# Two fused transformer layers on eight cores: first attention in query tiles of 256 with exponentials over three PSUM banks

## The reference, cut to what matters

```
# layer 0: full attention, 16 heads of 64, over all 4096 tokens of the sequence
q = quat_norm(quat_linear(x, qW, qb)); k = quat_norm(quat_linear(x, kW, kb)); v = quat_linear(x, vW, vb)
scores = einsum('bthd,bshd->bhts', q, k) * Dh ** -0.5 + mean(sin(J)) * 0.1
x = layernorm(x + quat_linear(softmax(scores) @ v, oW, ob))
# FFN: x and weight are quantized per block of 32 to fp6 (e2m3) with a block scale
x = layernorm(x + quantized(x) @ quantized(weight).T + bias)
# layer 1: windowed attention (256 keys), 16 heads on 2 key/value heads, then RWKV channel mixing
x = layernorm(x + local_attention(x) @ Wo + bo)
x = layernorm(x + sigmoid(xr @ Wr.T) * (square(relu(xk @ Wk.T)) @ Wv.T))
```

## Time and profile before

| | |
|---|---|
| median of 3 runs | 2056.3 us (2054.02 to 2269.13) |
| profiled execution | 2055.19 us; span of its slowest core 2053.7 us (cores 2044.7 to 2053.7) |
| TensorE busy | 1815.6 us, 88% of the span |
| ScalarE busy | 1616.9 us, 79% |
| VectorE busy | 1067.1 us, 52% |
| GpSimd busy | 406.4 us, 20% |
| stage B, 1088 steps | 1154 us |
| bridge | 134 us |
| stage C | 454 us |

### The profile page before, as it was taken

The page is one execution under the profiler, slowest core; times in us unless marked ns, Lnnn a source line. Parts: engine busy times, 40 slices in busy tenths (PEclk is TensorE's granted clock), DMA queues, the critical chain, the costliest instruction groups (busy, mean ns, idle before and its releaser), DMA issues.

```text
span 2053.7 us, 43415 instructions; the slowest of 8 cores (2044.7 to 2053.7 us)
## 1 busy us (share of the span) xinstructions
PE 1815.6 (88%) x14874; PEld 809.2 (39%) x15022; DVE 1067.1 (52%) x1568; ACT 1616.9 (79%) x2212; POOL 406.4 (20%) x271
## 2 busy tenths in 40 slices
PE   4999998888888989989989989899888799999995
PEld 2444444333222323323223322233345465556553
DVE  5655652476232244622254423464384568888873
ACT  2344339999999999999999999999624677887872
POOL 3000000000001000110000100001010267766775
PEclk9999999999999999999999999999999699999998
DMA  7323211100411010020101112202633301111111
GB/s 103 83 41 73 41 31 56 40 27 6 131 42 60 6 44 22 19 78 4 47 4 37 41 38 42 53 17 61 157 60 75 73 23 43 43 51 45 43 43 42
DMA packets 59731, 100.01 MB, mean 49 GB/s; under 512 B 21489, under 2 KB 42097, under 8 KB 58114
## 3 DMA queue, kind: packets, MB, share of 16 engines
q1 hardware_dynamic: 37010, 66.72, 10.0%
q0 software_dynamic: 22512, 30.51, 8.7%
HBM read 88.86 MB, written 22.02 MB: 54 GB/s over the span
## 4 chain that ended last, share of the span: by engine, by line
ACT 43%; PE 31%; issue 16%; DVE 6%; POOL 1%; DMA 1%; ACTq 1%; DVEq 0%; POOLq 0%
ACT TE L756 40%; PE PALL L1155 13%; PE PALL L1295 7%; PE PALL L1262 2%; PE PALL L1332 2%; PE PALL L1342 1%; PE PALL L1211 1%; PE PALL L1313 1%; DMA TE<-XF 1%; DVE SMALL L1102 1%; DVE TY L1089 1%; ACTq L755 1%; POOL TY L679 1%; PE PALL L1377 1%; DVE TY L1035 1%
## 5 line engine op out<-in xcount | busy, mean ns | idle before, releaser
L756 ACT ACTIVATE TE<-PALL,BIASB 128x1024 bf16<-128x1024 f32 x1088 | 1131.9, 1112 | 22.1 <-PE PALL L1168 11.9
L1168 PE MATMUL PALL<-TE,TY 64*128 64x512 bf16 (+1 forms) x2560 | 425.6, 351 | 117.0 <-ACT TE L756 115.7
L1184 PE MATMUL PALL<-TE,TY 128*64 128x512 bf16 (+1 forms) x2560 | 339.1, 357 | 0.7 <-ACT TE L756 0.7
L1193 PE MATMUL PALL<-TE,TY 128*64 128x512 bf16 x2176 | 325.7, 379 | 0.0
L1168 PEld LDWEIGHTS PALL<-TE,TY 64*128 64x128 bf16 x2560 | 123.0, 93 | 513.0 <-issue 511.5
L1028 DVE COPY TY<-PALL 128x512 f32<-128x512 f32 (+1 forms) x40 | 24.5, 612 | 345.3 <-PE PALL L1193 345.3
L771 ACT ACTIVATE TY<-PALL,SMALL 128x384 bf16<-128x384 f32 x272 | 155.9, 584 | 48.1 <-DVE SMALL L1063 47.5
L703 ACT ACTIVATE TX<-PALL,BIASB 128x512 f32<-128x512 f32 (+1 forms) x104 | 66.2, 658 | 148.4 <-PE PALL L1155 147.0
L611 POOL TENSOR_TENSOR TX<-TX 128x1024 f32<-128x1024 f32 x17 | 40.0, 2356 | 657.1 <-DVE TY L954 657.1
L1155 PE MATMUL PALL<-TE 128*128 128x512 bf16 (+1 forms) x692 | 143.9, 368 | 21.5 <-DMA TE<-XF 20.8
L1193 PEld LDWEIGHTS PALL<-TE,TY 128*64 128x64 bf16 x2176 | 120.3, 110 | 107.4 <-issue 7.3
(11 more groups left out here) (136 smaller groups left out, 2277.3 us busy)
## 6 DMA issues: line engine op xcount, KB each, us to landing
TE<-WOD SPq DMA_DIRECT2D x5, 2048.0 KB, 8.1
TX<-XST SPq DMA_DIRECT2D x17, 512.0 KB, 3.4
TY<-Y2SP POOLq DMA_DIRECT2D x17, 512.0 KB, 3.5
YOUT<-TY SPq DMA_DIRECT2D x17, 512.0 KB, 2.6
TE<-FWD SPq DMA_DIRECT2D x4, 2048.0 KB, 9.7
Y2SP<-TY SPq DMA_DIRECT2D x17, 256.0 KB, 2.0
TE<-XF POOLq DMA_DIRECT2D x8, 512.0 KB, 10.2
TY<-XF POOLq DMA_DIRECT2D x8, 512.0 KB, 9.4
```

The costliest lines, as they stand in the source:

```text
L756: s.activation(EXPS(m), PB(2 * (m % 2), 0, 1024), AF.Exp, bias=BIASB[:, 63:64], scale=0.125).then_inc(*up("exp", m))
L1168: op = t.matmul(PB(2 * (m % 2) + hh, x * w, w), KB(c, (s * k + x) * 128, 128, 64 * hh, 64), QB(c, 0, w, 64 * hh, 64), start=True, stop=Tru ...
L1184: t.matmul(PB(6, 0, w)[64 * hh:64 * hh + 64, :], VB((s + d) * k + x, (2 * c + hh) * 64, 64), EXPS(m + d)[:, hh * 512 + x * w:hh * 512 + x ...
L1193: op = t.matmul(PB(7, 0, 512)[64 * hh:64 * hh + 64, :], ONEB, EXPS(m + d)[:, hh * 512:hh * 512 + 512], start=(first and d == 0), stop=(las ...
```

## The change

- Queries of layer 0's attention go in nine tiles: one of 128 and eight of 256. Stage A keeps the old tiles under the name `ATILES`.
- The work is cut into 2176 units of 512 score columns (with 256 queries: 128 keys, both heads). A step is three units, 1536 columns in three banks (0 to 2, and 3 to 5), and one exponential; there are 726 steps. `EXPS` is a ring of 4.
- `scores(m)` has six matmuls of 256 columns. Unit 2 of a step has both of its heads in one bank; its second head waits, on the counter `third`, until the first one's matmul is complete.
- Numerators and denominators share bank 6 (256 columns each); `pv` goes by units. When the last unit of a (tile, c) is through, the rest of that iteration's units is put off to the next iteration (`pv_plan`).
- The products have one bank, 7, in stage B. Both chunks' first halves are done, then both chunks' second halves; `z1` and `z2` are done by half. `quant` is done in two parts. WB is loaded in halves of 1 MB, each as soon as that half has been used for the last time. Q tiles are loaded two tiles ahead, into two sets of buffers.
- `att_out` copies both parts in one instruction of 512 columns.
- The last tile has two chunks, so the bridge has two, and the last 512 tokens' `pre` are done as blocks of 256, 128 and 128.

```diff
-TILES = [(2048, 128), (0, 512), (512, 512), (1024, 512), (1536, 512)]
-STEPS = [(T, c, s) for T, (a, w) in enumerate(TILES) for c in range(8) for s in range(32 * w // 512)]
-NST = len(STEPS)
-RING = 6
+TILES = [(2048, 128)] + [(256 * i, 256) for i in range(8)]
+BUNITS = [(T, c, k) for T, (a, w) in enumerate(TILES) for c in range(8) for k in range(32 * w // 256)]
+NB = len(BUNITS)
+NST = (NB + 2) // 3
+RING = 4
+def pv_plan():
+    out, at, cut = {}, 0, False
+    for n in range(NST + 8):
+        avail = min(3 * (n - 1), NB)
+        if n % 2:
+            end = avail
+        elif cut:
+            end = min(3 * (n - 2), NB)
+        else:
+            end = max([u + 1 for u in range(at, avail) if is_last(u)], default=at)
+        cut = False
+        while at < end and not cut:
+            out.setdefault(n, []).append(at)
+            cut = is_last(at)
+            at += 1
+    return out
...
+    def tile(T, s):
+        n = TILES[T][1] // 128
+        for j in range(n):
+            put("sp", max(s - 24, 0), "xld", T, j)
+            put("pool", s - 2, "xb", T, j)
+            for nh in (0, 1):
+                e = s + 8 * (n * nh + j)
+                for i in range(4):
+                    put("pe", e + 2 * i, "o", T, j, 4 * nh + i)
+                put("dve", e + 7, "z1", T, j, nh)
+            put("act", e + 11, "r1", T, j)
+            put("dve", e + 12, "n1", T, j)
+        f = s + 16 * n + (6 if n == 2 else 14)
+        quant(T, 0, f - 9.5, f - 6.5)
+        if n == 2:
+            quant(T, 1, f + 4, f + 9.5)
+        for j in range(n):
+            ffn(T, j, f + 18 * j)
+        for nh in (0, 1):
+            put("sp", s + 8 * n * (nh + 1) - 1, "wld", T, "f", nh)
+            put("sp", f + 18 * n - 9 + 8 * nh, "wld", T + 1, "o", nh)
...
+    for T in range(L):
+        s = max(free, BASE[T + 1] + 8)
+        s += s % 2
+        free = tile(T, s) + (12 if T == 0 else 4)
...
+        def cols_of(u, hh):
+            return ((0, 512), (256, 768), (1024, 1280))[u % 3][hh]
...
-                s.activation(EXPS(m), PB(2 * (m % 2), 0, 1024), AF.Exp, bias=BIASB[:, 63:64], scale=0.125
+                s.activation(EXPS(m), PB(3 * (m % 2), 0, 1536), AF.Exp, bias=BIASB[:, 63:64], scale=0.125
...
             def scores(m):
                 if m >= 2:
                     t.wait_ge(*at("exp", m - 2))
-                for x in range(k):
-                    for hh in (0, 1):
-                        op = t.matmul(PB(2 * (m % 2) + hh, x * w, w), KB(c, (s * k + x) * 128, 128, 64 * hh, 64),
-                                      QB(c, 0, w, 64 * hh, 64), start=True, stop=True, tile_position=(64 * hh, 0))
+                for r, hh in (((2, 0), (0, 1), (0, 0), (1, 1), (1, 0), (2, 1)) if n == 3 else ((0, 0), (0, 1))):
+                    u = 3 * m + r
+                    T, c, k = BUNITS[u]
+                    w = TILES[T][1]
...
+                    if (r, hh) == (2, 1):
+                        t.wait_ge(*at("third", m))
+                    for x in range(256 // w):
+                        op = t.matmul(PB(3 * (m % 2), cols_of(u, hh) + x * w, w),
+                                      KB(c, (k * 256 // w + x) * 128, 128, 64 * hh, 64), QB(T, c, 64 * hh, 64),
+                                      start=True, stop=True, tile_position=(64 * hh, 0))
+                    if (r, hh) == (2, 0):
+                        op.then_inc(*up("third", m))
                 op.then_inc(*up("sc", m))
+            def pv(u):
+                if u % 3 == 0:
+                    t.wait_ge(*at("exp", m))
+                if k == 0 and u:
+                    t.wait_ge(*at("pvn", *BUNITS[u - 1][:2]))
+                for a in (0, 256):
+                    for x in range(256 // w):
+                        for hh in (0, 1):
+                            e = cols_of(u, hh) + x * w
+                            op = t.matmul(PB(6, a, w)[64 * hh:64 * hh + 64, :],
+                                          ONEB if a else VB(k * 256 // w + x, (2 * c + hh) * 64, 64), EXPS(m)[:, e:e + w],
...
             def att_out(T, c):
-                v.tensor_copy(NM, PB(6, 0, w)).then_inc(*up("pvn", T, c))
-                    op = v.tensor_copy(DN, PB(7, 0, w))
+                v.tensor_copy(MQ[:, 0:2 * w].rearrange("p (x q) -> p x q", q=w),
+                              PB(6, 0, 512).rearrange("p (x q) -> p x q", q=256)[:, :, 0:w]).then_inc(*up("pvn", T, c))
...
             for n in range(NST + 8):
                 if n < NST:
                     scores(n)
-                if n % 2 and 3 <= n < NST + 2:
-                    pv(n - 3)
+                for u in PVP.get(n, ()):
+                    pv(u)
                 beside(n)
```

More of the change, by code:

```diff
@@ L86, in b_plan @@
-    for k in range(8):
[L87 to L109, removed]
+    def quant(T, j, b, b2):
+        put("dve", b, "quant", T, j, 0)
+        put("dve", b2, "quant", T, j, 1)
+    def ffn(T, j, f):
+        put("pe", f, "t", T, j)
+        put("dve", f + 1, "tev", T, j)
+        put("pool", f + 1, "xf", T, j)
+        for i in range(8):
+            put("pe", f + 2 + 2 * i, "f", T, j, i)
+        put("dve", f + 9, "z2", T, j, 0)
+        put("dve", f + 17, "z2", T, j, 1)
+        put("act", f + 21, "r2", T, j)
+        put("dve", f + 22, "n2", T, j)
+        put("sp", f + 22, "y2", T, j)
@@ L110, in b_plan @@
+    for k in range(8):
+        b = 4 + 10 * k
+        quant("w", k, b, b + 3)
+        put("pe", b + 8, "t", "w", k)
+        put("dve", b + 9, "tev", "w", k)
+        put("sp", max(b - 30, 0), "fw", k)
+    put("sp", 86, "fwst")
+    for nh in (0, 1):
+        put("sp", 88, "wld", 0, "o", nh)
+    free = 108
+    for T in range(L):
+        s = max(free, BASE[T + 1] + 8)
+        s += s % 2
+        free = tile(T, s) + (12 if T == 0 else 4)
     B = BASE[L]
-    put("pool", B + 100, "w1qkv")
@@ L112, in b_plan @@
-    put("sp", B + 220, "x2", 4)
-    for i in range(2):
-        put("sp", B + 230, "x2", i)
+    put("pool", B + 12, "w1qkv")
+    for i, at in ((4, 34), (0, 44), (1, 55), (2, 66)):
+        put("sp", B + at, "x2", i)
     E = NST + 8
-    put("sp", E, "wld", L, "f")
-    put("sp", E + 1, "x2", 2)
-    put("pool", E + 1, "wk")
[L119 to L125, removed]
@@ L127, in last, with prep @@
-    def last(j, o, z1, n1, q, z2, n2):
-        put("pool", NST - 8 + 2 * j, "xb", L, j)
+    for j in (0, 1):
+        put("sp", B + 20, "xld", L, j)
+        put("pool", NST - 8 + 2 * j, "xb", L, j)
+    put("sp", E, "wld", L, "f", 0)
+    put("sp", E + 1, "x2", 3)
+    put("pool", E + 1, "wk")
+    put("pool", E + 13, "w1o")
+    put("pool", E + 50, "wr")
+    def prep(i, e, d):
+        for n in range(10):
+            put("pe", e + d * n, "pre", *i, n)
+            put("dve" if n == 1 else "act", e + d * n + 0.5, "prev", *i, n)
@@ L129, in last @@
+    def last(j, o, z1, n1, q, f, z2, n2):
         for i in range(8):
             put("pe", o + 0.1 * i, "o", L, j, i)
-        put("dve", z1, "z1", L, j)
+            put("pe", f + 1.5 + 0.1 * i, "f", L, j, i)
+        for nh in (0, 1):
+            put("dve", z1 + 0.1 * nh, "z1", L, j, nh)
+            put("dve", z2 + 0.1 * nh, "z2", L, j, nh)
         put("act", z1 + 2.6, "r1", L, j)
         put("dve", n1, "n1", L, j)
-        put("dve", q, "quant", L, j)
+        quant(L, j, q, q + 0.1)
         put("pool", q + 8, "xf", L, j)
-        put("pe", q + 8.6, "t", L, j)
@@ L137, in last @@
[L137 to L140, removed]
+        put("pe", f, "t", L, j)
+        put("act", f + 1, "tev", L, j)
         put("act", z2 + 3, "r2", L, j)
@@ L143, in last, with back @@
         put("sp", n2, "y2", L, j)
[L145 to L154, removed]
+    def back(j, e):
         put("pe", e, "yt", L, j)
         put("act", e + 0.4, "yte", L, j)
-        prep((3, j), [e + 0.5 + 0.45 * n for n in range(10)])
+    prep((4, -1), E, 0.5)
+    last(0, E + 5, E + 8.6, E + 13.2, E + 17.2, E + 30, E + 36, E + 41)
+    last(1, E + 9, E + 12.2, E + 17.4, E + 26, E + 38, E + 44, E + 49)
+    prep((0, -1), E + 13, 1.7)
+    prep((1, -1), E + 34, 1.8)
+    back(0, E + 53)
+    prep((2, -1), E + 54, 1.7)
+    back(1, E + 71)
+    prep((3, 0), E + 72, 0.9)
+    prep((3, 2), E + 82, 0.5)
+    prep((3, 3), E + 88, 0.5)
     for e in plan:
-        plan[e] = {it: plan[e][it] for it in sorted(plan[e])}
+        steps = {}
+        for it in sorted(plan[e]):
+            steps.setdefault(int(it) if it < NST + 8 else it, []).extend(plan[e][it])
+        plan[e] = steps
     return plan
@@ L468, in _ @@
             y.dma_start(out=OBD, in_=OBROW[0:1, :]).then_inc(*up("obd", by=16))
[L469 to L470 removed]
+            for i in range(NA):
+                a, w = ATILES[q_tile(i)]
                 for h in range(2):
```

345 lines of the change are left out of this document (169 added, 176 removed).

## The result

The changed kernel takes 2140.2 us (median of 4 runs) where the kernel before took 2055.5: the ratio is 1.041, with a 95% interval of 1.039 to 1.043. It is slower by more than 2%, to which the forecast gave 0.35 (0.43 went to "within 2%"), and 5 us above the stated range. The profiled execution took 2137.45 us against 2055.19, 82 more. (In some runs the cores of one die are granted a lower clock and take some per cent longer; the ratios leave these runs out, and the text goes by ratios.)

A forecast was written before the change was run, and what follows sets the result against it. TensorE was taken as the bound beside a product part, a ring between TensorE and ScalarE elsewhere. 2055.2 + 26 (steps) + 24 (hand-offs) + 11 (late copies) + 1 (stage B's start) - 32 (bridge) = 2085 us; range 1985 to 2135.

The forecast's parts named there:

- the stated range: Whole kernel: 1985 to 2135 us, taking in rival 2's value and the nearly free wait on third at 0.10.
- the ring of exponential and scores: Stage B without a product part: exponential, answer, scores, V and ones, next exponential set the pace, 3.07 us a pair of steps.
- ScalarE's floor of 2.88: Stage B: exponentials at a pitch of 1.44 us, 2.88 a pair of steps, reached neither with nor without a product part.
- V and ones: TensorE's V and ones matmuls in stage B: 12 pairs and changes of tiling, 1.43 us in two steps.
- The bridge: The part with two chunks less and the last 512 tokens' blocks: from 134 to 102 us, -32 (bounds -24 and -38).
- Transfers: WB moved in halves, 17 times instead of 9, and q loads a tile ahead: cost nothing.
- The wait on `third`: Last score matmul of each step in stage B: stalls TensorE 0.25 us (bounds 0 and 0.30), scores hold it 0.68.
- 1180 + 24 in the forecast: Stage B: 1180 us for 363 pairs of steps against 1154 before, plus 24 for punctual hand-offs of bank 6.
- the hand-off of bank 6: Stage B, before a c's first V matmul: TensorE waits for the bank's copy, +24 us (bounds 0 and 40), late copies +11.
- late copies: Bank 6's copy behind quant on VectorE, about one place a tile, and a tight first tile: +11 us (bounds 0 and 50).
- Rival 2: Bank 6's copy queued behind quant on VectorE costs 50 to 60 us in place of 11: 2130 us; chance 0.20.
- Rival 3: Narrow matmuls cost a fixed 0.02 us a pair, 18 pairs in two steps: +131, 2215 us; chance 0.03.

The follow-up runs named there:

- e7: The changed kernel with each exponential over 1024 of the step's 1536 columns: 2125 us in the best run, ratio 1.038 (1.021 to 1.054) to the kernel before.
- e4: The changed kernel without quant's rounding to the fp6 grid, four of six VectorE instructions of each half left out: 2055 us, ratio 1.000 to the kernel before.
- e2: The changed kernel with the copy out of bank 6 done by ScalarE instead of VectorE: about 2089 us, ratio 1.017 to the kernel before.
- e5: The changed kernel with VectorE's copy out of bank 6 in its own buffer, put between single instructions of quant: 2082 us, ratio 1.013 to the kernel before.
- e1: The changed kernel with units cut by head, one head to a bank, and no wait on third: 2091 us, ratio 1.018 to the kernel before.
- e3: The changed kernel with one head to a bank and the bank 6 copy done by ScalarE: 2040 us, ratio 0.993 to the kernel before.
- e6: The changed kernel with one head to a bank, VectorE's copy between single instructions, weight chunks every 12 steps instead of 10: 2027 us, ratio 0.987 to the kernel before.

## Why the prediction was wrong

**Steps that held.** With a product part beside the attention TensorE is the bound (e7 shortens the exponentials, and these pairs stay at 3.22 us). Without one the ring of exponential and scores is, as forecast: 3.07 forecast, 3.11 measured. The prediction also said that ScalarE's floor of 2.88 is reached in neither kind of stretch; about a third of the pairs without a product did reach it (2.86). V and ones take 1.43 a pair of steps. The bridge went from 134 to 100, forecast 102. Transfers: no wait of TensorE for a half of WB is in the list, though the bytes that SP's queue moved rose from 67 to 84 MB. The halves of WB cost nothing.

**The wait on `third`**: mechanism right, size a little over. It holds a score group to 0.63 us, not 0.68: the stall is 0.20, not 0.25, and a pair with a product takes 3.22, not 3.33. The steps with the punctual hand-offs, 1180 + 24 in the forecast, came to 1174. This error of 30 us was in the kernel's favour, and it hides a part of the next one.

**The step that failed is "the hand-off of bank 6"**, in its second term: late copies, put at 11 us with bounds 0 and 50. It measured 102, the excess of the 46 pairs of steps above. It was mis-sized in two ways.
1. The late copies. I had seen that `att_out` could stand behind the second half of `quant`, in one place a tile, and called the first tile crowded. 20 copies were late: 8 up to 463 us, for 28 us of standing, and 12 in the tiles after, for 37. The normalization (line 1083) stands in that queue too, and no term had it; its 0.81 us were 2.8 in the five places of stage B in which GpSimd was adding, and four of the late copies stand behind one of these.
2. The clock. No term of the sum had it. In a stand or shortly after it the granted clock went to the lower level for 3.4 or 6.8 us; 102 us of stage B at half rate are at most 51 us of lost TensorE time. Of the 102 us of excess the stands of over 1 us take 72, which leaves some 30 for the clock and for all else.

**Rival 2 had the mechanism**, with a chance of 0.20, but its 2130 came near the measured 2140 by luck: it priced the late copies at 50 to 60 us, half of what they cost, and the steps, 30 us cheaper than forecast, made up for most of that. Its test, more than a third of the 72 hand-offs late by over 0.5 us, was not met: 20 were, 28%, but they cost 3.3 us of standing each on average, and the lower clock after most of them. Its number of late places (7 and a dozen) was about right. The weight against it, "VectorE is only 45% busy", was the mistake: in stage B of the changed kernel it is busy for 43%, and e4, which left out VectorE work alone, took away 84 us. What counts is the longest thing in the queue before the copy, not how full the queue is.

**Rival 3's price** (131 us) counts 0.02 us for all 18 pairs of matmuls, though 9 of them were there before; the 1.43 of V and ones shows that there is no such cost in any case.

**Is the cause settled?** Late hand-offs: shown three ways (e2 another engine copies, e4 the queue is shorter, e5 the copy is earlier in it), 50, 84 and 58 us, each with the wait and the lower clock going down together, and in e4 and e5 with the ordinary pairs unchanged. The wait on `third`: shown by e1, 49 us, all of it in the ordinary pairs, and it adds to the first (e3: 98). That the lower clock is a cost of its own and not a companion of the stands was not tried apart; only the sum above says so. What the 256-query tiles and the longer exponentials give in stage B is nothing even with both repaired as far as e6 does it: 1161 us against 1154, of which 36 still go to stands and the lower clock.

## What to carry to other kernels

When a change shortens the time between a buffer's last write and its next use, look up the longest instruction sequence that can stand before the release in the releasing engine's order, and price each meeting with the waiting engine's time and the time at a lower clock after it; a busy share of 50% says nothing about that. Cheaper work on an engine that is not the bound comes back as idle time: find out first, by the ring of waits, which engine's order sets the step. And give a buffer's release its own scratch space, so that it can be placed anywhere in its engine's order.

## What the runs showed of the hardware

A matmul of 256 columns that waits for the completion of an earlier one on the same engine is issued about 0.4 us after that one: the sixth weight load begins 0.41 us after the group's first. With four other matmuls between them 0.20 us of it stay visible (0.63 us for a score group; three pairs of 0.11 and a change of tiling of 0.10 would be 0.43).

VectorE's normalization of 128x1024 f32 took 0.79 to 0.81 us in the 11 places where GpSimd was idle, and 2.77 to 2.87 us in the 6 where GpSimd had just begun its 2.34 us addition (671.20 and 671.23 above). `att_out`'s last multiply (line 1122, 128x256 f32) took 2.0 to 2.3 us instead of 0.43 in 6 places of that kind. The copy out of PSUM was never stretched (0.69 at most, in 72). The Trainium skill (Advanced Engine Details and Errata, VectorE Performance Modes, Mode Summary) states that the second SBUF port of VectorE is shared with GpSimd, so that instructions of GpSimd and those of VectorE that use two ports block each other. The trace agrees as far as the blocking goes: the normalization above ended 0.55 us after GpSimd's addition did. Which port it was no run here shows.

In stage B of the changed kernel the granted clock fell from 2.4 to 1.2 GHz in, or within 2 us of the end of, 20 of the 24 stands of TensorE of over 1 us. These 20 lasted 1.7 to 5.8 us; after stands of 1.0, 1.35, 1.35 and once 2.7 us it did not fall. It stayed there for 3.4 or 6.8 us. It fell not once in stage B of the kernel before, whose longest stand for an exponential there was 1.1 us.
